# A graph layer whose row gathers all go through GpSimd: two groups of rows fetched by SyncE, and another order of the last steps

## The reference

```python
h = jnp.maximum(_layernorm(x, axis=-1), 0.0)
out = h @ W_root + bias
for r in range(8):
    m = (edge_type == r).astype(x.dtype)
    msg = h[src] @ W[r] * m[:, None]
    agg = segment_sum(msg, dst, num_segments=n)
    cnt = segment_sum(m, dst, num_segments=n)
    out = out + agg / jnp.maximum(cnt, 1.0)[:, None]
return x + out
```

## Time and profile before, and how to read it

| | us |
|---|---|
| median of three runs | 1027.13 |
| profiled execution, its own time | 1027.01 |
| its span, first to last instruction | 1025.3 |
| POOL busy | 764.0 (75%) |
| TensorE matmuls busy | 769.2 (75%) |
| VectorE busy | 704.9 (69%) |
| ScalarE busy | 414.4 (40%) |
| mean granted TensorE clock | 0.715 |

### The profile page before, as it was taken

One profiled execution on the slowest core, in us unless ns is written; L12 is line 12 of the kernel. 1 busy time (PEld: TensorE's weight loads), 2 busy tenths in 40 slices (PEclk: granted clock), 3 DMA queues, 4 the chain that ended last, 5 costly groups with the idle time before them and its releaser, 6 DMA issues.

```text
span 1025.3 us, 15294 instructions
## 1 busy us (share of the span) xinstructions
PE 769.2 (75%) x4342; PEld 630.8 (62%) x4342; DVE 704.9 (69%) x2301; ACT 414.4 (40%) x821; POOL 764.0 (75%) x820
## 2 busy tenths in 40 slices
PE   0487787877878867778778678688687787776886
PEld 0376675665766756656656567566566575565676
DVE  7797988778776666575765765656746656657585
ACT  8984352342342433423424324334234243252341
POOL 7777777777777777777777777777777777777772
PEclk9996767676677676766766766766767667667678
DMA  9694222222222222222222222222222222222221
GB/s 284 182 213 97 54 60 54 57 57 56 55 57 55 59 54 59 54 58 57 57 57 57 54 59 54 56 57 57 56 58 54 60 54 55 58 57 54 59 55 34
DMA packets 51608, 71.42 MB, mean 70 GB/s; under 512 B 13843, under 2 KB 36662, under 8 KB 51526
## 3 DMA queue, kind: packets, MB, share of 16 engines
q0 software_dynamic: 25632, 52.55, 20.4%
q1 hardware_dynamic: 25894, 17.90, 6.9%
HBM read 63.99 MB, written 6.40 MB: 69 GB/s over the span
## 4 chain that ended last, share of the span: by engine, by line
POOL 63%; issue 21%; DVE 6%; PE 5%; DMA 1%; DVEq 0%; ACT 0%; POOLq 0%; ACTq 0%
POOL hg L499 63%; PE acc L1500 1%; DVE onehot L1004 1%; DVE ring L1018 1%; PE fin L1531 1%; DMA hg<-h_table,src_i 1%; DVE x_all L1102 1%; PE fin L1620 1%; PE zp L1630 1%; DVE blk L1262 0%; DVE blk L1265 0%; DVE fin L1053 0%; DVE t_stats L755 0%; PE zp L1520 0%; PE acc L1504 0%
## 5 line engine op out<-in xcount | busy, mean ns | idle before, releaser
L499 POOL DMA_INDIRECT hg<-h_table,src_i x777 | 737.8, 950 | 237.1 <-issue 234.7
L1500 PE MATMUL acc<-onehot,hg 128*128 128x96 f32 (+1 forms) x1602 | 409.3, 368 | 206.3 <-DMA hg<-h_table,src_i 171.1
L1500 PEld LDWEIGHTS acc<-onehot,hg 128*128 128x128 f32 x1602 | 320.0, 248 | 286.3 <-issue 218.8
L1018 DVE TENSOR_TENSOR ring<-ring,acc 128x512 f32 x267 | 182.0, 682 | 243.6 <-PE acc L1507 242.3
L622 ACT ACTIVATE hT<-zp 128x116 f32<-128x116 f32 x50 | 13.4, 267 | 527.2 <-PE zp L1538 527.2
L1504 PE MATMUL acc<-onehot,ones_bf 128*128 128x96 bf16 (+1 forms) x801 | 204.4, 255 | 0.0
L1004 DVE TENSOR_SCALAR onehot<-iota,key_f 128x96 f32<-128x96 f32 (+1 forms) x801 | 196.8, 293 | 10.9 <-issue 2.4
L1531 PE MATMUL fin<-w_sb,blk 128*116 128x128 f32 x800 | 173.4, 388 | 0.0
L1531 PEld LDWEIGHTS fin<-w_sb,blk 128*116 128x116 f32 x800 | 156.3, 280 | 12.1 <-issue 11.9
L1102 DVE SCALAR_TENSOR_TENSOR x_all<-fin,inv,x_all 116x128 f32<-116x128 f32 x400 | 139.2, 348 | 14.4 <-DVE x_all L1092 0.5
L612 ACT ACTIVATE loop_far<-iota,loop_key 96x256 f32<-96x256 f32 x267 | 134.0, 502 | 34.0 <-PE acc L1507 22.0
(11 more groups left out here) (150 smaller groups left out, 374.1 us busy)
## 6 DMA issues: line engine op xcount, KB each, us to landing
hg<-h_table,src_i POOLq DMA_INDIRECT x777, 2.5
out<-x_all SPq DMA_DIRECT2D x53, 58.0 KB
x_all<-in_x SPq DMA_DIRECT2D x7, 384.0 KB, 7.8
h_table<-h_all SPq DMA_DIRECT2D x7, 384.0 KB
h_all<-h_table SPq DMA_DIRECT2D x5, 504.0 KB
x_all<-in_x SPq DMA_DIRECT2D x5, 504.0 KB
w_sb<-in_L_gnn_W SPq DMA_DIRECT2D x1, 512.0 KB
h_all<-h_table SPq DMA_DIRECT2D x1, 448.0 KB
```

The lines of the kernel that those rows point to most:

```text
L499: nc.gpsimd.indirect_dma_start(out=hg[:, slot_of(t), :], out_offset=None, in_=x if g < XG else table, in_offset=bass.IndirectOffsetOnAxis( ...
L1018: nc.vector.tensor_tensor(ring[:, :, :, at], ring[:, :, :, at], acc[:, q, :, :].rearrange("p a (r n) -> p a r n", r=R), ALU.add).then_inc( ...
L1500: nc.tensor.matmul(both[:, 0, :, a:e], hg[:, slot, :], hot.rearrange("p (r n) -> p r n", r=R), start=(j == 0), stop=(j == n - 1), skip_gro ...
```

## The change

- Groups 210 and 265 get six slots of `hg` of their own, and POOL issues no gather for them. SP fetches their 768 rows one by one: it copies the 128 indices of a tile into one partition (in `e_rows_i`, no longer needed), loads 16 of them into registers and issues 16 row copies with computed addresses. These 48 batches stand between the stores of blocks 8 to 46. TensorE waits for all 384 rows of such a group at its first tile.
- The indices of the first tile are also loaded as 128 words by SP, ahead of everything; POOL's first gather waits for them alone, the second for the old path. Six memsets go from POOL to VectorE.
- In the tail TensorE sums groups 265 and 266 each before the `add_up` that stood ahead of it, and VectorE adds them to the ring in that order. `add_last_sum(b2)` comes after the last window. The last window's place is worked out in a later iteration.
- Two scratch tiles of the general path (not taken on these inputs) move into `hg`.

```diff
+FETCHED = (209, 264)
+FETCH = 16
+FETCH_FROM = 7
+FETCH_TO = 46
...
-        hg = sb("hg", [P, 2 * IT, F])
+        hg = sb("hg", [P, 2 * IT + len(FETCHED) * GT, F])
...
+            sp.dma_start(src_i[:, 0:1], src[0:P].rearrange("(e a) -> e a", a=1)).then_inc(first_src_in, 16)
             sp.dma_start(src0_rows_i[:, :], src[0:WHOLE * P].rearrange("(t e) -> t e", e=P)).then_inc(src0_in, 16)
...
-            with sp.Fori(0, BLOCKS - 1) as b:
-                store(b, BLK)
-            store(BLOCKS - 1, LASTN)
+            late = fetched_tiles()
+
+            def fetch_sources(k):
+
+                part = max(n for n, first in enumerate(PART_GROUPS) if first <= late[k] // GT)
+                sp.wait_ge(src_ready, part + 1)
+                sp.dma_start(late_src[:, k % 2 * P:(k % 2 + 1) * P], src_i[:, late[k]:late[k] + 1]).then_inc(late_src_in, 16)
+
+            def fetch_rows(c):
+
+                k, at = divmod(c * FETCH, P)
+                regs = [sp.alloc_register(f"late{c}_{n}") for n in range(FETCH)]
+                sp.wait_ge(late_src_in, 16 * (k + 1))
+                sp.load(regs, late_src[0:1, k % 2 * P + at:k % 2 * P + at + FETCH])
+                for n in range(FETCH):
+                    row = sp.snap(regs[n], donate=True, min_val=0, max_val=N - 1)
+                    sp.dma_start(hg[at + n:at + n + 1, slot_of(late[k]), :], table[bass.ds(row, 1), :]).then_inc(
+                        fetched[k // GT], 16)
+                if at == 0 and k + 1 < len(late):
+                    fetch_sources(k + 1)
+
+            batches = len(late) * P // FETCH
+            done = 0
+            for b in range(BLOCKS):
+                store(b, LASTN if b == BLOCKS - 1 else BLK)
+                if b == FETCH_FROM:
+                    fetch_sources(0)
+                while done < min(batches, batches * (b + 1 - FETCH_FROM) // (FETCH_TO - FETCH_FROM)):
+                    fetch_rows(done)
+                    done += 1
...
-            for a, v in ((0, 0), (1, PAD_DST), (2, PAD_TYPE)):
-                nc.gpsimd.memset(e_rows_i[:, a, CHUNKS - 1, :], v).then_inc(pads, 1)
-            nc.gpsimd.memset(x_all[:, LC, :], 0.0).then_inc(pads, 1)
-            for nodes in (x_all, h_all):
-                nc.gpsimd.memset(nodes[:, BLOCKS - 1, :], 0.0).then_inc(pads, 1)
...
-            pool.wait_ge(src0_i, 1)
+            pool.wait_ge(first_src_in, 16)
             for t in range(TILES):
                 g = t // GT
                 if t % GT == 0:
                     if g == XG:
                         pool.wait_ge(h_stored, H_STORES)
+                if t == 1:
+                    pool.wait_ge(src0_i, 1)
...
-                    if user_before(g) >= 0:
+                    if user_before(g) >= 0 and g not in FETCHED:
                         pool.wait_ge(group_summed, user_before(g) + 1)
+                if g in FETCHED:
+                    continue
...
-                    else:
+                    elif g not in FETCHED:
                         pe.wait_ge(gathered[slot], 16 * uses_to(i * IT + t))
+                    elif j == 0:
+                        pe.wait_ge(fetched[FETCHED.index(g)], 16 * GT * P)
...
-                add_last_sum(b1)
                 add_group(EARLY + 4, 4, at_last[1])
+                add_last_sum(b1)
                 dve.wait_ge(bad_sum, 1)
                 nc.vector.tensor_scalar(flag[:, :], badT, 1.0, None, ALU.min).then_inc(flag_ready, 1)
-                add_last_sum(b2)
                 add_group(ENDG, 0, at_last[2])
                 make_last_block(b3)
                 dve.wait_ge(blk_made, 2 * b3 + 2)
                 add_group(ENDG + 1, 1, at_last[3])
-                finish_sums(b3, GALL)
-                make_last_window(b3, window)
+                make_last_window(b3, *window)
                 last_inverses(2, b3, 1)
+                add_last_sum(b2)
                 add_last_terms(b3)
...
-                add_up(b1)
                 pe.wait_ge(tail_inv_step, 2)
                 sums_of(ENDI, 4, GT)
+                add_up(b1)
                 pe.wait_ge(bad_ready, 1)
                 pe.wait_ge(group_added, EARLY + 3)
                 nc.tensor.matmul(badT, bad1[:, :], ones[:, 0:1], start=True, stop=True).then_inc(bad_sum, 1)
-                add_up(b2)
                 pe.wait_ge(tail_inv_step, INV_STEPS + 2)
                 sums_of(ITERS - 1, 0, GT)
+                add_up(b2)
                 sums_of(ITERS - 1, 1, GT)
```

More of the change, by code:

```diff
@@ L56, in start_of, with fetched_tiles @@
     return t * P if t <= WHOLE else WHOLE * P + (t - WHOLE) * RAW
+def fetched_tiles():
+    return [g * GT + j for g in FETCHED for j in range(GT)]
 def window(j):
@@ L213, in rgcn @@
         g_put = sb("g_put", [P, 1], i32)
-        g_h = sb("g_h", [P, VW])
         g_low = sb("g_low", [P, P])
@@ L263, in rgcn @@
         gathered = [sem(f"gathered{j}") for j in range(2 * IT)]
+        fetched = [sem(f"fetched{g}") for g in FETCHED]
+        late_src_in = sem("late_src_in")
         group_summed, group_added = sem("group_summed"), sem("group_added")
@@ L306, in slot_of @@
         def slot_of(t):
+            if t // GT in FETCHED:
+                return 2 * IT + fetched_tiles().index(t)
             return t if t < FIRST * GT else (t - FIRST * GT) % (DEEP * GT)
         def uses_to(t):
-            return 1 if t < FIRST * GT else (t - FIRST * GT) // (DEEP * GT) + (2 if slot_of(t) < FIRST * GT else 1)
+            return sum(slot_of(u) == slot_of(t) for u in range(t + 1))
         def from_x(i, q):
@@ L1177, in iteration @@
                             places_in_order()
+                            places_of_last_window()
                         if q == 2:
@@ L1269, in make_last_block, with places_of_last_window, make_last_window @@
                 make_last_half(b, 1)
-            def last_window():
-                at = dve.alloc_register("last_window")
-                dve.wait_ge(window_ready, 1)
-                dve.load([at], at_i[0:1, ITERS - 1, PLACES - 1:PLACES])
-                return dve.snap(at, donate=True, min_val=BLK, max_val=2 * BLK - WINN)
-            def make_last_window(b, window):
-                cols, slot = bass.ds(window - BLK, WINN), bass.ds(window + PRE + (b % RING - 1) * BLK, WINN)
+            def places_of_last_window():
+                in_block, in_ring = (at_i[:, ITERS - 1, k:k + 1] for k in (PLACES - 2, PLACES - 1))
+                nc.vector.tensor_scalar(in_ring, dev[0:1, GALL - 1:GALL], float(BLK), float(2 * BLK - WINN), ALU.max,
+                                        ALU.min).then_inc(window_ready, 1)
+                dve.wait_ge(window_ready, 1)
+                nc.vector.tensor_scalar(in_block, in_ring, -float(BLK), None, ALU.add).then_inc(window_ready, 1)
+                dve.wait_ge(window_ready, 2)
+                nc.vector.tensor_scalar(in_ring, in_ring, float(PRE + ((BLOCKS - 1) % RING - 1) * BLK), None,
+                                        ALU.add).then_inc(window_ready, 1)
+            def last_window():
+                at = [dve.alloc_register(f"last_window{k}") for k in range(2)]
+                dve.wait_ge(window_ready, 3)
+                dve.load(at, at_i[0:1, ITERS - 1, PLACES - 2:PLACES])
+                slot = PRE + ((BLOCKS - 1) % RING) * BLK
+                return (dve.snap(at[0], donate=True, min_val=0, max_val=BLK - WINN),
+                        dve.snap(at[1], donate=True, min_val=slot, max_val=slot + BLK - WINN))
+            def make_last_window(b, in_block, in_ring):
+                cols, slot = bass.ds(in_block, WINN), bass.ds(in_ring, WINN)
+                finish_sums(b, GALL)
                 h_b = tail_hT[:, b - ENDB, cols].unsqueeze(1).to_broadcast([P, R, WINN])
```

33 lines of the change are left out of this document (19 added, 14 removed).

## The result

| | before | after |
|---|---|---|
| median of five runs, us | 1027.13 | 1021.9 |
| lowest and highest, us | 1026.34 to 1029.66 | 1019.85 to 1022.15 |
| ratio to before, 95% interval | | 0.9938 [0.9927, 0.9948] |
| profiled execution, its own time; its span | 1027.01; 1025.3 | 1021.90; 1020.0 |
| POOL busy, us | 764.0 | 757.4 |

The account below looks back on a forecast made before the run. POOL's 801 indirect gathers, 1.253 us each, were taken to bound the kernel. Gathers -3.76, tail order -1.8 and start +0.2 sum to -5.36 us: 1021.8 us against the median, range 1019.2 to 1024.6.

Parts of the forecast that it names:

- Six gathers fewer, group 210: -3.76: Mid-kernel on POOL: leaving out group 210's three gathers moves all later gathers and the tail 3.76 us earlier.
- Group 265: 0: In the tail: dropping group 265's gathers is worth 0 by itself, since TensorE was not waiting for that data.
- Row traffic: 0: While SP copies rows: this traffic does not lengthen POOL's gathers, so it costs 0 us.
- the rival's mechanism: Row traffic lengthens POOL's gathers beside SP's batches; 0.05 us each would give 1032.1 us; chance 0.15, half of it slower.
- SP's issue: 0.34 us per row: On SP's queue: 0.26 us issue plus 0.08 register work per row, 261 us for 768, within its waiting time.
- That SP can fall behind: Rival on SP's queue: the rows come too late, decided above 1.02 us per row; chance 0.03.
- The start: +0.2, with gather 34 still held by group 2: At the start: POOL's earlier first gather gains 0, as group 2 still holds gather 34; later loads cost 0.2 us.
- The order of the tail: -1.8: At the end: summing 265 and 266 ahead of block products gains 1.9 us, less unseen waits, so 1.8.
- the bound of -2.2: Tail order's most favourable limit: at best 2.2 us gained; the other limit was 0.
- The clock helps: a rival, 0.17: In the tail: shorter idle time keeps TensorE's clock up in the last products, giving 1019.3 to 1021 us; chance 0.17.
- Its signs: Trace checks across the kernel that would show the forecast right, such as 795 gathers at 948 ns with 0.30 us gaps.
- The many-small-transfers warning: For SP's row copies: small transfers should be coalesced; 2.0 us fixed cost paid serially would give near 1.76 ms.

Follow-up runs that it names:

- e4: The change, but POOL gathers all 801 tiles and TensorE uses those, while SP still fetches 768 unused rows: 1241.12 us, 1.0085 of the kernel before.
- k2: The change without SP's row fetches, POOL gathering all 801 tiles, new start and tail kept: 1226.52 us, 0.9980 of the kernel before.
- g1: The change with groups 131 and 210 fetched instead of 210 and 265, and the old start: 1339.51 us, 1.0767 of the kernel before.
- k1: The change, unedited, run again on a slow chip: 1231.53 us, 1.0014 of the kernel before.
- e2: The change with the tail order of the kernel before on TensorE and VectorE: 1235.04 us, 1.0037 of the kernel before.
- f2: The change with the tail order of the kernel before, repeated on another slow chip: 1245.06 us, 1.0015 of the kernel before.
- e1: The change with only group 210 fetched, POOL gathering group 265 again: 1231.13 us, 1.0003 of the kernel before.
- k4: The change with only group 210 fetched and the old start: 1229.80 us, 0.9995 of the kernel before.

## Why the prediction was right, and where only its sum was

The forecast was 1021.8 and the range 1019.2 to 1024.6; the result is 1021.9. The mechanism was right in its two main terms, the gathers and the order; that the sum was met to 0.1 us is luck. By its own steps:

- **Six gathers fewer, group 210: -3.76.** Right, in mechanism and size: -3.74 between tiles 627 and 631, and nothing of it is lost up to tile 792.
- **Group 265: 0.** The trace of after agrees, and no run on that chip tested it. Without the fetch the last gather of 265 would begin at 1000.54 - 2.40 = 998.1 and land by 1000.6, and group 267's would begin at 1002.12 + 3.76 = 1005.9 and land by 1008.4; TensorE takes them up at 1003.25 and 1009.46. Both would be in time.
- **Row traffic: 0.** Right on the chip of the result (947 ns beside the batches in both traces). Not a property of the chip type: on the two slow chips of e4 and k2 together the rows cost 12 to 15 us, and not by longer gathers, which was the rival's mechanism (they stay at 950 ns there): POOL waits for sums 116 times in e4 and 93 in k2, 204 us for 182 (the waits on "remote" counted in).
- **SP's issue: 0.34 us per row** (0.37 in another place of it). Too small: 0.41 measured for the copies and 0.49 with the register load of 16 values, which I had left out of the price. Of the 0.41, 0.228 is the copy and 0.07 the register work; the rest lies between the instructions. It cost nothing, since SP had 1.02 us per row. That SP can fall behind was right in kind: on a slow chip a row takes about 1 us (1.08 in a pair of batches of g1), and g1, with 0.82 us per row at hand, waits 112.5 us for the rows. k1 does not: at some 0.97 per row on average it issues its last one at 1188 us, and TensorE takes up group 265 only at 1211.8.
- **The start: +0.2, with gather 34 still held by group 2.** Wrong in mechanism and too small. The new issue puts the x loads 0.48 us later (1.75 for 1.27), of which I had let the vanished wait for memsets pay 0.3; that wait stood behind the first two loads of x and pays nothing to them. The first also takes longer to land (median 3.2 us for 2.8), and VectorE begins 0.96 later. The normalised table is stored later, and it is gather 25, not 34, that waits, 2.52 us for it. The new first gather runs into that wait, not into group 2's. I had looked for who holds POOL at the start and had found only the wait that was the longest before, not the one that was just in time. It measured +0.59 in one trace of each kernel. Between gathers 34 and 200 POOL loses another 0.8 us to longer gathers, before any row is fetched, for which I have no cause that a run shows; it may be what differs between any two executions.
- **The order of the tail: -1.8.** The add of 266 is 1012.22 - 1007.72 = 4.50 earlier, of which 2.40 had come in with the gathers: 2.10 by the order, for the 1.9 of the working. Right, and near the bound of -2.2, since no new wait appeared; e2 and f2, which undo the order, give the same 2.10 back. The add of 267 follows 3.41 later, as the 3.40 of the working had it.
- **The clock helps: a rival, 0.17.** Half of it came true: the last products at full clock take 2.00 for 3.76, and the last terms start 5.53 earlier where the add of 267 is 4.49 earlier: -1.04. The products at 984 us still fell into a slow stretch (3.57 for 16). This part is luck even so: of eleven traces of the new order the first half of these products ran at full clock in five and mostly at half clock in six, behind the same 1.28 us of idle time.
- **Its signs.** 795 gathers, their length and gaps, no wait for SP's rows, and the add of 266 less than 5 us after 265 (3.08) came as said. SP's rows at 0.3 to 0.4 us (0.41, or 0.49 with the load), gather 34 held, the last gather 7.3 us earlier (6.15) and the add of 267 some 5.4 earlier (4.49) did not: the start and the early slip took 1.2 us of the last two.

So the sum: +0.59 + 0.8 (start and early slip) - 3.74 - 2.10 - 1.04 = -5.5 at the start of the last terms (traced: -5.53, of which 0.2 is lost behind them: the span is 5.3 shorter), where I had +0.2 - 3.76 - 1.8 = -5.36. The total was met because two errors cancelled: the start and the early slip were 1.2 us dearer, and the tail and its clock 1.3 us better. With the last products at half clock the same sum gives some 1022.8 us (an estimate: 1021.9 and the 0.9 us that such traces take more to the last terms). A reader should trust the terms for group 210 and for the order of the tail, and not the one for the start, and not count on the clock.

The many-small-transfers warning of the Trainium skill (*DMA: Bandwidth & Descriptors*, Rules for kernel authors) did not decide here. The 768 transfers of 0.5 KB were issued from 224 to 943 us at 0.41 us each, and TensorE summed group 265 at 1003 without a wait for them, so they did not land one after the other at more than (1003 - 224) / 768 = 1.0 us each. No run here grouped them, so what grouping would save on the slow chips is open.

## What to carry to other kernels

Follow the same tile or group through the traces before and after and look at the difference at five or six places: it tells at once which part of a change pays where, and it showed here that a prediction met to 0.1 us stood on two cancelling errors. Then look for the same stretch in every other trace you have, of whatever experiment: the tail's 2.10 us came back in all of them, and the clock's 1.04 only in some. Work taken from the bounding engine is worth its full time only while that engine is the bound, so ask of a helper queue not only whether it has idle time but at what price per instruction it would become the bound (1.02 us per row for the change, 0.82 for g1, where it was passed). At a start or an end, look for the waits of length near zero: they are the next ones.

## What the runs showed of the hardware

- The same kernel takes 1027 us on one chip and 1230 to 1243 on three others. In the trace of k2 there gathers have the same length (950 ns), and TensorE stands between matmuls for some 192 us (125.5 + 66.9 at the two lines of the sums) where the profile names no cause (4.7 at L1560 in after on the first chip). What sets these chips apart stays open.
- On such a chip SP's issue of a row takes about 1 us while the other engines work (1.08 in a pair of batches of g1), 0.93 us while TensorE alone stands still, and 0.45 us while all of them wait, as long as on the first chip (14.32 and 14.33 us for 32).
- The same 16 last products, behind the same 1.28 us of idle time, run at a granted clock of 1.00 in one execution (e1, 2.00 us) and 0.50 in another (k4, 3.76 us).
- A register load of 16 values by SP takes 1.2 to 1.3 us; a row copy with a computed address 228 ns of issue and some 70 ns of register work, 0.41 us from one to the next.
- A transfer of 0.5 KB as 128 words, put ahead of the loads, took 2.1 us to land, and the loads of x behind it came in 0.96 us later (statistics at 5.03 for 4.07; 0.4 to 0.7 later with it than without it on the slow chips).
